# Bias product and the patch's last 48 rows in fp32r, with rounded part and remainder stacked along the contraction

## The reference

```
tokens = patches(64, 64, 2352) @ W.T + b         # 8 x 8 patches of 28 x 28 x 3, 128 features
h  = concat([class_token, tokens]) * pos_embed   # (64, 65, 128)
h += attention(layernorm(h))     # 8 heads of 16; q, k through relu; scores divided by the key's sum; softmax
f  = layernorm(layernorm(h)) (scale, bias)
out = h + swiglu_shared(f) + shared_out_b + cnt @ expert_out_bias
        + sum_e comb[:, e] * (swiglu_expert(f) @ expert_out_weight[e].T)
```

## Time and profile before

| | |
|---|---|
| median of three runs | 537.16 us (536.97 to 537.72) |
| profiled execution | 538.47 us, its span 536.6 us |
| PE busy | 489.3 us (91%) |
| DVE busy | 321.2 us (60%) |
| ACT busy | 184.1 us (34%) |
| POOL busy | 173.8 us (32%) |
| mean granted TensorE clock | 0.939 |
| patch product, L421 | 137.6 us, 288 instructions |
| patch's tail, L426 | 9.0 us, 16 instructions |
| bias product, L589 | 9.0 us, 16 instructions (and 0.7 us for the class tokens) |

### The profile page before, as it was taken

One profiled execution on the slowest core, in us unless ns is written; L12 is line 12 of the kernel. 1 busy time (PEld: TensorE's weight loads), 2 busy tenths in 40 slices (PEclk: granted clock), 3 DMA queues, 4 the chain that ended last, 5 costly groups with the idle time before them and its releaser, 6 DMA issues.

```text
span 536.6 us, 6981 instructions
## 1 busy us (share of the span) xinstructions
PE 489.3 (91%) x2194; PEld 331.9 (62%) x2194; DVE 321.2 (60%) x869; ACT 184.1 (34%) x342; POOL 173.8 (32%) x213
## 2 busy tenths in 40 slices
PE   5899997999999999999999999999697869898974
PEld 2355556665775578557755776567576646786562
DVE  0043356375856586658765776667677758646652
ACT  0035115432273218411742255215631553122220
POOL 6013201120462037202711183107311821224443
PEclk9989996899999999999999999999979978969976
DMA  8995660055004600461045200000100010000001
GB/s 340 352 410 188 203 223 0 0 177 184 1 20 165 197 1 6 136 200 41 0 136 164 79 0 20 0 0 1 21 0 1 1 21 0 1 1 1 20 1 22
DMA packets 14413, 44.71 MB, mean 83 GB/s; under 512 B 1721, under 2 KB 7090, under 8 KB 14386
## 3 DMA queue, kind: packets, MB, share of 16 engines
q1 hardware_dynamic: 12882, 42.39, 23.4%
q10 hardware_dynamic: 1504, 1.99, 1.1%
HBM read 42.24 MB, written 2.13 MB: 83 GB/s over the span
## 4 chain that ended last, share of the span: by engine, by line
PE 68%; DVE 15%; issue 7%; DMA 4%; POOL 3%; ACT 2%; ACTq 1%; DVEq 0%; POOLq 0%; SPq 0%
PE acc L421 20%; PE scores L482 6%; PE O L508 5%; PE B L407 4%; DMA bq_row<-in_bq_row 3%; DVE z_nat L1080 2%; PE scores L620 2%; PE C L620 2%; PE B L445 2%; PE C L621 1%; PE acc L655 1%; PE C L559 1%; PE C L622 1%; PE B L464 1%; PE scores L621 1%
## 5 line engine op out<-in xcount | busy, mean ns | idle before, releaser
L421 PE MATMUL acc<-x_main,w_patch 128*128 128x512 f32 x288 | 137.6, 607 | 5.9 <-DMA w_patch<-in_w_patch 5.9
L421 PEld LDWEIGHTS acc<-x_main,w_patch 128*128 128x128 f32 x288 | 53.2, 194 | 49.3 <-issue 41.4
L1567 POOL TENSOR_TENSOR prod<-prod 128x512 f32<-128x512 f32 (+1 forms) x33 | 42.6, 1292 | 35.2 <-DVE prod L1292 35.1
L839 ACT ACTIVATE probs<-shift 128x512 f32<-128x512 f32 x32 | 20.4, 637 | 80.8 <-DVE shift L1132 80.8
L508 PEld LDWEIGHTS O<-v_bd,probs_t 128*128 128x128 f32 x256 | 33.6, 200 | 22.7 <-issue 12.1
L1560 POOL TENSOR_TENSOR hidden_lo<-silu,hidden_hi 128x512 fp32r<-128x512 f32 (+1 forms) x18 | 20.9, 1164 | 74.8 <-ACT hidden_hi L839 74.7
L482 PE MATMUL scores<-k_bd,q_mask 128*128 128x260 f32 x128 | 38.4, 425 | 5.8 <-DVE shift L1132 3.1
L508 PE MATMUL O<-v_bd,probs_t 128*128 128x64 f32 (+1 forms) x256 | 35.6, 284 | 5.0 <-ACT probs_t L839 5.0
L1128 DVE TENSOR_REDUCE row_max<-scores 128x8 f32<-128x520 f32 x32 | 22.3, 698 | 28.8 <-PE scores L482 28.4
L482 PEld LDWEIGHTS scores<-k_bd,q_mask 128*128 128x128 f32 x128 | 23.3, 203 | 18.7 <-issue 7.9
L1529 POOL TENSOR_TENSOR p_cls<-exp_cls,row_rec 128x16 f32<-128x16 f32 x16 | 3.5, 222 | 94.0 <-DVE row_rec L1147 94.0
(11 more groups left out here) (251 smaller groups left out, 1016.7 us busy)
## 6 DMA issues: line engine op xcount, KB each, us to landing
x_main<-in_x_main SPq DMA_DIRECT2D x48, 768.0 KB, 4.2
out_tokens<-y_out SPq DMA_DIRECT2D x16, 128.0 KB, 2.5
w_patch<-in_w_patch ACTq DMA_DIRECT2D x6, 192.0 KB, 9.7
prod<-in_w_eout SPq DMA_DIRECT2D x2, 512.0 KB
x_tail<-in_x_tail SPq DMA_DIRECT2D x8, 96.0 KB, 3.3
silu<-in_w_in SPq DMA_DIRECT2D x2, 256.0 KB
hidden<-in_rows ACTq DMA_DIRECT2D x1, 256.0 KB, 16.1
w_attn<-in_w_attn ACTq DMA_DIRECT2D x1, 256.0 KB, 17.5
```

The costliest lines, as they stand in the source:

```text
L421: last = mm(acc[:, :], w_patch[:, j, :], x_main[:, j, :], start=(j == 0), stop=False)
L839: return nc.scalar.activation(dst, src, func, **kw)
L1567: q.tensor_tensor(p[r, 0, :], p[r, 0, :], p[r, 1, :], ALU.add).then_inc(tree1_done.sem, 1)
```

## The change

Both products are turned from fp32 into fp32r, with the two parts of an operand stacked along the contraction, so that one product takes several terms.

The tail: x_tail is loaded with 112 rows: the 48, 16 of zeros, and the same 48 again. w_tail holds the rounded weights in rows 0 to 47 and their remainder in rows 64 to 111, made once by VectorE. ScalarE rounds all of x_tail (`tail_high`), GpSimd subtracts (`tail_low`, 48 rows). TensorE multiplies 112 rows (rounded x by both parts of the weights) and 48 rows (remainder of x by rounded weights). `tail_high(g+2)` stands in ScalarE's body(g) behind exps(g,1) and, in the bodies that aren't lean, ahead of probs_out(g,0); `tail_low(g+2)` in GpSimd's behind the two hidden_low. For groups 0 and 1 they stand ahead of body 0. SP loads the first tail ahead of the pieces, and each later one once GpSimd is done with the one before.

The biases: the counts are small whole numbers and need no remainder, so count holds them twice (18 columns) and bias_s the rounded biases above their remainders (18 rows). The second half of count is a second multiply in `choose`; bias_s is made once in body 0, by two instructions each on ScalarE and GpSimd. The buffer reserved for DMA descriptors is made smaller.

```diff
@@ sync
             def load_x(g):
+                if isinstance(g, int) and g == 0:
+                    load_tail(0)
                 for i, (a, b) in enumerate(PIECES):
...
-                need(sp, acc_full, g - 1)
+                if not (isinstance(g, int) and g == 0):
+                    load_tail(g)
+
+            def load_tail(g):
+                need(sp, xtlo_done, g - 1)
                 src = A["x_tail"][bass.ds(g, 1), :, :].rearrange("g p t -> (g p) t")
                 sp.dma_start(x_tail[:, :], src).then_inc(x_in[-1].sem, 16)
@@ tensor
-                        need(pe, x_in[-1], g)
-                        mm(acc[:, :], w_patch_tail[:, :], x_tail[:, :], start=False, stop=True)\
+                        need(pe, xtlo_done, g)
+                        mm(acc[:, :], w_tail[:, :], x_tail_hi[:, :], start=False, stop=False)
+                        mm(acc[:, :], w_tail[0:NTAIL, :], x_tail_lo[:, :], start=False, stop=True)\
                             .then_inc(acc_full.sem, 1)
...
-                    mm(dst, out_bias[:, :], count_t[:, 0:n], start=False, stop=True).then_inc(sht_full.sem, 1)
+                    mm(dst, bias_s[:, :], count_t[:, 0:n], start=False, stop=True).then_inc(sht_full.sem, 1)
...
-            pe.wait_ge(w_first.sem, FIRST)
+            pe.wait_ge(wt_done.sem, 2)
             patch(0, NMAIN, NMAIN + 1)
@@ scalar
+            def tail_high(g):
+                need(act, x_in[-1], g)
+                need(act, acc_full, g - 1)
+                go(x_tail_hi[:, :], x_tail[:, :]).then_inc(xthi_done.sem, 1)
...
+            tail_high(0)
             act.wait_ge(cpe.sem, 1)
             go(hn_cls_t[:, :], B1[:, 0:128]).then_inc(cact.sem, 1)
             natural(0, 0)
             normed_t(0)
+            tail_high(1)
...
+                go(bias_hi[:, :], out_bias[:, :]).then_inc(whi_done.sem, 1)
+                go(bias_own[:, 0, :], out_bias[:, :], scale=const[0:BIAS_ROWS, C_BIAS + 1:C_BIAS + 2]).then_inc(whi_done.sem, 1)
...
                 exps(g, 1)
+                if not lean:
+                    tail_high(g + 2)
                 if lean and nxt:
                     natural(g + 1, 1 - par)
                 probs_out(g, 0)
@@ vector
-                v.tensor_tensor(cnt, e_row[r, 0:S].rearrange("p (t a) e -> p t a e", a=2), bcast(g_sel[r, 0:T], EG),
-                                ALU.mult).then_inc(count_done.sem, 1)
+                for first in (0, EXPERTS + 1):
+                    cnt = count[r, 0:T, first:first + EXPERTS].rearrange("p t (a e) -> p t a e", e=EG)
+                    v.tensor_tensor(cnt, e_row[r, 0:S].rearrange("p (t a) e -> p t a e", a=2), bcast(g_sel[r, 0:T], EG),
+                                    ALU.mult).then_inc(count_done.sem, 1)
...
             dve.wait_ge(w_first.sem, FIRST)
+            v.tensor_copy(w_tail[:, :], w_patch_tail[:, :]).then_inc(wt_done.sem, 1)
+            dve.wait_ge(wt_done.sem, 1)
+            low = slice(64, TAIL_ROWS)
+            v.tensor_tensor(w_tail[low, :], w_patch_tail[low, :], w_tail[low, :].bitcast(F32), ALU.subtract)\
+                .then_inc(wt_done.sem, 1)
@@ gpsimd
+            def tail_low(g):
+                need(pool, xthi_done, g)
+                need(pool, acc_full, g - 1)
+                q.tensor_tensor(x_tail_lo[:, :], x_tail[0:NTAIL, :], x_tail_hi[0:NTAIL, :].bitcast(F32), ALU.subtract)\
+                    .then_inc(xtlo_done.sem, 1)
+
+            tail_low(0)
             q.memset(neg_half[:, :], -0.5).then_inc(pool_init.sem, 1)
...
             norm_scale1(0)
+            tail_low(1)
...
+                if has_patch(g):
+                    tail_low(g + 2)
                 class_value(g, 0)
@@ host layouts
-        "x_tail": xg[:, main:],
+        "x_tail": np.concatenate([xg[:, main:], np.zeros((GROUPS, gap, TOK), xg.dtype), xg[:, main:]], 1),
...
-        "w_patch_tail": wp[main:],
+        "w_patch_tail": np.concatenate([wp[main:], np.zeros((gap, D), wp.dtype), wp[main:]], 0),
...
-    nc = bacc.Bacc("TRN2", target_bir_lowering=False, num_devices=1)
+    nc = bacc.Bacc("TRN2", target_bir_lowering=False, num_devices=1, dynamic_dma_scratch_size=2048)
```

More of the change, by code:

```diff
@@ L48 @@
 NGATE = 2 + EXPERTS
+BIAS_ROWS = 2 * (EXPERTS + 1)
+TAIL_ROWS = 64 + NTAIL
 ATTN_EPS = 1e-6
@@ L55 @@
 C_ID, C_PAR, C_TRI, C_THR, C_HROW, C_HMASK, C_PMASK = 0, 128, 130, 146, 150, 158, 286
-C_HEAD = 302
-NCONST = 310
+C_HEAD, C_BIAS = 302, 310
+NCONST = 312
 V_POS, V_TOK_B, V_BK, V_BV, V_SCALE, V_BIAS = NCONST, NCONST + 64, NCONST + 65, NCONST + 66, NCONST + 67, NCONST + 68
@@ L75, in shape_constants @@
     c[:, C_HEAD:C_HEAD + HEADS] = (p[:, None] // DH) == np.arange(HEADS)
+    c[:, C_BIAS] = np.where(p <= EXPERTS, 1, -1)
+    c[:, C_BIAS + 1] = p > EXPERTS
     return c
@@ L109, in vit_tower @@
         w_patch = sb("w_patch", [128, NMAIN, D])
-        w_patch_tail = sb("w_patch_tail", [NTAIL, D])
+        w_patch_tail = sb("w_patch_tail", [TAIL_ROWS, D])
+        w_tail = sb("w_tail", [TAIL_ROWS, D], F32R)
         bq_row = sb("bq_row", [128, D])
@@ L118, in vit_tower @@
         w_eout_hi = sb("w_eout_hi", [128, HC, EXPERTS, D], F32R)
-        out_bias = sb("out_bias", [EXPERTS + 1, D])
+        out_bias = sb("out_bias", [BIAS_ROWS, D])
+        bias_s = sb("bias_s", [BIAS_ROWS, D], F32R)
+        bias_hi = sb("bias_hi", [BIAS_ROWS, D], F32R)
+        bias_own = sb("bias_own", [BIAS_ROWS, 2, D])
         w_attn = sb("w_attn", [128, 4, D])
@@ L128, in vit_tower @@
         x_main = sb("x_main", [128, NMAIN, TOK])
-        x_tail = sb("x_tail", [NTAIL, TOK])
+        x_tail = sb("x_tail", [TAIL_ROWS, TOK])
+        x_tail_hi = sb("x_tail_hi", [TAIL_ROWS, TOK], F32R)
+        x_tail_lo = sb("x_tail_lo", [NTAIL, TOK], F32R)
         h_t = [sb(f"h_t{i}", [128, TOK]) for i in range(2)]
@@ L181, in vit_tower @@
         e_top = sb("e_top", [128, TILES * 2, EG])
-        count = sb("count", [128, TILES, EXPERTS + 1])
+        count = sb("count", [128, TILES, BIAS_ROWS])
         e_keep = sb("e_keep", [128, TILES, EXPERTS])
@@ L186, in vit_tower @@
         comb = sb("comb", [128, TILES, EXPERTS])
-        count_t = sb("count_t", [EXPERTS + 1, TOK])
+        count_t = sb("count_t", [BIAS_ROWS, TOK], F32R)
         silu = [sb(f"silu{i}", [128, TOK]) for i in range(2)]
@@ L246, in vit_tower @@
         x_used = ev("x_used", len(PIECES))
+        xthi_done, xtlo_done, wt_done = ev("xthi_done"), ev("xtlo_done"), ev("wt_done", 0)
         stored = ev("stored", 32)
@@ L573, in counts @@
                 for t in range(tiles):
-                    last = nc.tensor.transpose(count_bank(g)[0:EXPERTS + 1, t * 128:t * 128 + rows], count[0:rows, t, :],
+                    last = nc.tensor.transpose(count_bank(g)[0:BIAS_ROWS, t * 128:t * 128 + rows], count[0:rows, t, :],
                                                ident[0:rows, 0:rows])
@@ L721, in body @@
                     gates(0, TILES, 128)
-                    pe.wait_ge(wlo_done.sem, 4)
+                    pe.wait_ge(wlo_done.sem, 6)
                 if last:
@@ L1549, in weights_low @@
                         .then_inc(wlo_done.sem, 1)
+                pool.wait_ge(whi_done.sem, 6)
+                q.tensor_scalar(bias_own[:, 1, :], bias_hi[:, :].bitcast(F32), const[0:BIAS_ROWS, C_BIAS:C_BIAS + 1], None,
+                                ALU.mult).then_inc(wlo_done.sem, 1)
+                pool.wait_ge(wlo_done.sem, 5)
+                q.tensor_tensor(bias_s[:, :], bias_own[:, 0, :], bias_own[:, 1, :], ALU.add).then_inc(wlo_done.sem, 1)
             def z_low(g, n):
@@ L1650, in row @@
         return np.asarray(a).reshape(1, -1)
+    bias = np.concatenate([L0_ffn_expert_out_bias, row(L0_ffn_shared_out_b)], 0)
+    gap = 64 - NTAIL
     layouts = {
         "x_main": xg[:, :main].reshape(GROUPS, NMAIN, 128, TOK).transpose(0, 2, 1, 3),
-        "x_tail": xg[:, main:],
+        "x_tail": np.concatenate([xg[:, main:], np.zeros((GROUPS, gap, TOK), xg.dtype), xg[:, main:]], 1),
         "w_patch": wp[:main].reshape(NMAIN, 128, D).transpose(1, 0, 2),
-        "w_patch_tail": wp[main:],
+        "w_patch_tail": np.concatenate([wp[main:], np.zeros((gap, D), wp.dtype), wp[main:]], 0),
         "w_attn": np.stack([t(L0_attn_Wq), t(L0_attn_Wk), t(L0_attn_Wv), t(L0_attn_Wo)], 1),
@@ L1665 @@
                     .transpose(1, 0, 2, 3),
-        "out_bias": np.concatenate([L0_ffn_expert_out_bias, row(L0_ffn_shared_out_b)], 0),
+        "out_bias": np.concatenate([bias, bias], 0),
         "const": np.concatenate([shape_constants(), pos[1:].T, col(L0_tok_b), col(L0_attn_bk), col(L0_attn_bv),
```

5 lines of the change are left out of this document (2 added, 3 removed).

## The result

| | before | after |
|---|---|---|
| median of 6 runs, us | 537.07 (536.65 to 537.72) | 540.13 (538.0 to 540.91) |
| profiled execution, us (span) | 538.47 (536.6) | 540.22 (538.3) |
| busy PE / DVE / ACT / POOL, us | 489.3 / 321.2 / 184.1 / 173.8 | 479.2 / 328.7 / 188.3 / 184.5 |

The medians are 3.1 us apart; the ratio is 1.0049, 95% interval 1.0028 to 1.0070, or 2.6 us (1.5 to 3.8). Slower, then, by half a percent. Forecast was 537.9, no change that can be told; 540.13 lies inside the range, near its slow end. TensorE is busy 10 us less, and the time is longer.

A forecast was written before the change was run, and what follows sets the result against it. TensorE was taken to bound the kernel up to prob_v(3), VectorE from there to z_transpose. Tail -2.7, ScalarE +2.5, lock +2.25, bias -2.75, count +0.3, start +1.1 sum to +0.7 on 537.16: 537.9 us, range 534.6 to 540.6.

The forecast's parts named there:

- rival C: Body 0's start stalls longer because x_tail(1) lands at 41.5, not 39.4: +2.1, 540.0; chance 0.26 with the dear 112-row pass.
- a dear 112-row pass: Tail product's 112-row pass costs as much as a 48-row one: +1.9, 539.8; shares chance 0.26 with rival C.
- Tail, 0.40 a body: Two fp32r passes replace the fp32 tail pair on TensorE, 0.27 paid for few rows: 0.40 saved each, -2.7 in all.
- ScalarE's copy, +0.5 a body: tail_high ahead of probs_out(g,0) delays prob_v(0) by 0.5 in bodies 1 to 5: +2.5.
- Port lock, +0.45 a body: VectorE's e_row waits for GpSimd's tail_low, delaying prob_v(1) in bodies 1 to 5: +2.25.
- Bias, -2.75: One fp32r bias product saves 0.6: -1.25 over bodies 1 to 5, -1.2 in bodies 6 and 7, -0.3 class group.
- Start, +1.1: Larger loads ahead of bq_row +0.4; tail_high(1) waiting for x_tail(1) delays k_t and, through it, v_proj: +0.7.
- The body, 56.0 from 55.7: Steady body length: 55.7 plus 0.5 ScalarE and 0.45 lock, less 0.4 tail and 0.25 bias, gives 56.0.
- second count multiply: Extra VectorE multiply in choose, on the chain in body 7 and twice in the epilogue: 3 x 0.1 = +0.3.
- A: The port lock between VectorE and GpSimd costs nothing: -2.25, 535.6, faster; chance 0.20.
- D: Nothing of the change is on the path, gain and loss both covered: 537.2; chance 0.06.
- B: Tail and bias products save what their columns say, no 0.27 at few rows: 535.4, faster; chance 0.12.

The follow-up runs named there:

- both_late: Changed kernel with ScalarE's tail_high(g+2) and GpSimd's tail_low(g+2) both moved to where their queues are idle; 536.60 us, ratio 0.9976 to the kernel before.
- best_rows128: Whole change, both copies late, start rearranged, VectorE's loop at its old place and length, tail zero-padded to 128 rows in both passes; 529.79 us, ratio 0.9829 to kernel before.
- hi_late: Changed kernel with only ScalarE's tail_high(g+2) moved behind hidden_high(1) and route_exp; 538.82 us, one execution.
- lo_late: Changed kernel with only GpSimd's tail_low(g+2) moved behind class_value(g,0); 539.90 us, one execution.
- run again: The changed kernel run once more, unchanged; 539.89 us, ratio 1.0037 to the kernel before.
- bias_only: Kernel before with the bias part of the change alone, tail as before; 540.52 us, one execution.
- tail_only: Kernel before with the tail part of the change alone, bias product as before; 537.06 us, one execution.
- placed: Whole change, but w_tail made on GpSimd and one multiply writing both count halves, so VectorE's loop keeps its old place and length; 535.19 us, ratio 0.9965 to kernel before.
- after_pad82: Changed kernel with 82 waiting instructions on VectorE ahead of its loop, moving the loop to 324 to 663; 540.12 us.

## Why the prediction was right, and what it missed

The range held the time and most of the terms were right; but what made the kernel slower is a step that the prediction doesn't have. Its slow end came from rival C and a dear 112-row pass, and neither put the time there; that 540.13 lies inside is luck. Term by term:

- *Tail, 0.40 a body*: right. 1.58 became 1.18; both_late against the kernel before, less the bias part, gives 0.38 to 0.41 in bodies 2, 4 and 5. The 0.27 for few rows was also right in kind, and best_rows128 shows it to be a matter of rows: it went both for 112 and for 48. That the 112-row pass would cost what a full one does was wrong by 0.1 (0.41 and not 0.31), and the 48-row pass cost less than the 0.50 given to it (0.42): two errors that cancel, so the 0.40 to the hundredth is in part luck.
- *ScalarE's copy, +0.5 a body*: right; 0.49 by hi_late, and the 0.47 wait at prob_v(0) with the releaser named.
- *Port lock, +0.45 a body*: right in kind, too high in size; 0.29 by lo_late. (The trace before showed the lock on e_top in six bodies, 1 to 6, and not in seven: in body 7 hidden_lo has ended 1.2 us before e_top starts, and e_top takes 0.19.) Both copies on their own account would be 0.95 a body and are 0.80: prob_v(1) came at 174.42 - 168.29 = 6.13 behind prob_v(0), where 173.4 - 167.08 = 6.3 had been worked out.
- *Bias, -2.75*: -0.25 a body was forecast, 0.32 measured; the growth of the wait ahead of z_transpose, 0.35 forecast, was 0.34.
- *Start, +1.1*: 0.4 was forecast by way of bq_row and 0.7 behind tail_high(1). The second mechanism was right in the profiled pair, at 1.1; run again shows that it vanishes when TensorE is late by itself. The first was not: VectorE's first instruction behind bq_row starts at 24.66 in both kernels, and the 0.40 is the wait for x_main, a term that was put at 0. That wait is no steady cost of the change either: 1.25 in run again, 0.76 in bias_only, whose tail is the old one. The prediction took this stretch as fixed.
- *The body, 56.0 from 55.7*: 55.86 from 55.77, so +0.1 and not +0.3.

With the measured sizes the sum is 5 x 0.49 + 5 x 0.29 - 7 x 0.38 - (5 x 0.32 + 1.2 + 0.3) + 0.3 + 1.54 = 0.0, and with the stall (body 3, +3.6) 3.6; measured 2.6 (1.5 to 3.8). The terms 1.2, 0.3 and 0.3 are the prediction's and were not measured apart, and the 1.54 is the least certain: at the first score of body 1 the changed kernel is 0.74 behind, and 1.1 with body 0's own tail taken out.

The step that failed is the second count multiply, "3 x 0.1 = +0.3". It was priced as VectorE time, 0.1 where VectorE is late and nothing in bodies 1 to 5, and not as instructions in a loop that jumps back: it puts two multiplies and one more waiting instruction into the loop of two bodies. tail_only, one place later and no longer, has no stall; bias_only, at the same start and three longer, has it. (A loop at 242 with the old length, which would part the shift from the three instructions in the changed kernel itself, was not run.) The prediction names TensorE, DMA, the queues and the port as resources, but not the stream of instructions. The profile before could have raised the question: it has an instruction queue (q14), and no packet of it between 225 and 370 us, in which the loop runs its second time. Of this the Trainium skill says (Runtime: NRT & Kernel Launch, Instruction fetch mechanics) that a taken branch to a place outside the fetched window forces a fetch before execution goes on; the runs agree, at 2.3 to 2.7 us in each of the seven kernels whose loop ends at 580 or 581. It gives blocks of 16 KiB, or 256 instructions; a packet of this queue was 8 KB (18 packets, 0.15 MB over the span), which by the same measure is 128. As an estimate from that page's figure: with an edge at 577 to 579, the loops without a stall lie in three pieces of 128, or in two of 256, and those with one reach into one more. The places fit a grain of either size, so the grain stays open.

Of the rivals, A (lock at no cost) and D are out by lo_late and hi_late, B by the 0.41 and 0.43 of the tail's passes. C had the sign and the size, 540.0, but not the mechanism: x_tail(1) landed at 39.7 and not at 41.5.

## What to carry to other kernels

A loop can have a cliff at its jump back: here one of 336 instructions jumped back free from places 240 and 241, and five places or three instructions more cost 3.2 to 3.6 us. Count a loop's instructions, waits included, and after each change look for "issue" ahead of the first instruction behind the jump. Put work added to a queue where that queue is idle, not where its input is ready; and where a contraction is short, try it padded with zeros to all 128 rows before trying to save rows.

## What was not expected of the hardware

- Time moves with TensorE's clock from one execution to the next, and only in certain stretches. The kernel before took 530.73 us at a granted clock of 0.969 and 541.83 at 0.937 on one chip. Bodies 1, 2 and 4 repeat within 0.05 us; body 0, in which TensorE has gaps, took 53.12 us at 0.90 in run again and 58.01 at 0.82 in bias_only, without anything of its own work changed by as much. The windows of the two:
```profile
50.75:103.87 53.12, 48.06 (x198) 31.03 (x199) 25.61 (x72) 22.96 (x41) 15.93 (x17) 0.90 0.40 128
```
```profile
49.25:107.26 58.01, 53.60 (x198) 35.40 (x199) 25.63 (x72) 22.45 (x40) 14.95 (x16) 0.82 0.35 112
```
  A change of 1 us is therefore read from the bodies, not from the median.
- A stall of 2.6 us on VectorE costs 3.6 in the profiled pair (3.2 to 3.6 over the eight profiles): TensorE waits 2.08 itself and then runs some 3.4 us at the half clock, which loses it another 1.7.
- In body 1 of the changed kernel z_transpose waits 1.33 instead of the 0.98 of bodies 2 to 5; in placed and after_pad82 that body is 0.35 to 0.45 shorter. VectorE stands 0.46 ahead of attn_nat (133.19), with nothing but its own last instruction to wait for, where the other bodies have 0.10. It looks like a smaller stall of the same kind, and was not tested by itself.
